# A linear attention product on two 64-row halves of the array, a value block in one piece, and one weight split on GpSimd

## What is computed

```python
# cross attention: the value and output weights are folded into one product
out = softmax(qp @ kp.T * scale) @ vp @ Wo.T
# linear attention, 16 heads of 32
q, k = relu(rmsnorm(q)), relu(rmsnorm(k))
kv = einsum('bhnd,bhne->bhde', k, v)
out = einsum('bhnd,bhde->bhne', q, kv)
out = out / (einsum('bhnd,bhd->bhn', q, k.sum(axis=2)) + eps)[..., None]
x = x + out @ W_out + b_out
# experts: 4 of 256 hidden columns
hid = silu(x @ Wg[e]) * (x @ Wu[e])
```

## Time and profile before

| | |
|---|---|
| median of 3 runs | 527.33 us (526.98 to 527.74) |
| the profiled execution | 527.25 us |
| its span | 525.1 us |
| TensorE busy | 520.9 us, 99% of the span |
| VectorE, ScalarE, GpSimd busy | 374.2, 243.3 and 245.3 us |

### The profile page before, as it was taken

One profiled execution on the slowest core, in us unless ns is written; L12 is line 12 of the kernel. 1 busy time (PEld: TensorE's weight loads), 2 busy tenths in 40 slices (PEclk: granted clock), 3 DMA queues, 4 the chain that ended last, 5 costly groups with the idle time before them and its releaser, 6 DMA issues.

```text
span 525.1 us, 6996 instructions
## 1 busy us (share of the span) xinstructions
PE 520.9 (99%) x2536; PEld 434.4 (83%) x2536; DVE 374.2 (71%) x615; ACT 243.3 (46%) x391; POOL 245.3 (47%) x159
## 2 busy tenths in 40 slices
PE   9999999999999999999999999999999999999997
PEld 8888888888888888888888888888888888988885
DVE  5673677876667766567878644999967477739996
ACT  4743434745535444453554534656645332562210
POOL 3735006331211322224244243338519948888993
PEclk9999999999999999999999999999999999999999
DMA  8721233232422223322232212242250312751102
GB/s 307 315 70 52 81 85 116 104 137 82 149 92 80 81 92 144 143 104 81 102 139 80 82 40 73 81 169 80 98 183 1 120 42 90 253 200 60 61 1 80
DMA packets 17607, 57.10 MB, mean 109 GB/s; under 512 B 2083, under 2 KB 2595, under 8 KB 16806
## 3 DMA queue, kind: packets, MB, share of 16 engines
q1 hardware_dynamic: 17286, 56.27, 30.5%
q10 hardware_dynamic: 288, 0.39, 0.2%
HBM read 54.55 MB, written 2.10 MB: 108 GB/s over the span
## 4 chain that ended last, share of the span: by engine, by line
PE 99%; DVE 0%; issue 0%; POOL 0%; POOLq 0%
PE bank L1463 28%; PE bank L1581 11%; PE bank L1592 11%; PE bank L1582 11%; PE bank L1594 11%; PE bank L1583 11%; PE bank L1593 11%; PE bank L1513 2%; PE bank L1453 1%; PE bank L1731 1%; PE bank L1474 1%; PE bank L1488 0%; PE bank L1720 0%; PE bank L1782 0%; DVE xs L1444 0%; PE bank L1749 0%
## 5 line engine op out<-in xcount | busy, mean ns | idle before, releaser
L575 POOL TENSOR_TENSOR cn_l<-raw_n,cn_h 128x1024 fp32r<-128x1024 f32 x32 | 77.7, 2428 | 185.5 <-ACT cn_h L757 185.5
L775 ACT COPY ring<-bank 128x512 f32<-128x512 f32 x64 | 37.7, 589 | 148.3 <-PE bank L1583 148.1
L1100 DVE TENSOR_TENSOR top<-top,bank 128x512 f32<-128x512 f32 x60 | 41.1, 685 | 86.4 <-ACT ring L775 86.3
L1581 PE MATMUL bank<-qk_h,ct_h 128*128 128x512 f32 x256 | 99.8, 390 | 0.0
L1583 PE MATMUL bank<-qk_h,ct_l 128*128 128x512 f32 x256 | 99.6, 389 | 0.0
L1582 PE MATMUL bank<-qk_l,ct_h 128*128 128x512 f32 x256 | 99.6, 389 | 0.0
L1592 PE MATMUL bank<-ph,cn_h 128*128 128x512 f32 x256 | 99.6, 389 | 0.0
L1593 PE MATMUL bank<-pl,cn_h 128*128 128x512 f32 x256 | 99.6, 389 | 0.0
L1594 PE MATMUL bank<-ph,cn_l 128*128 128x512 f32 x256 | 99.6, 389 | 0.0
L1581 PEld LDWEIGHTS bank<-qk_h,ct_h 128*128 128x128 f32 x256 | 48.0, 188 | 10.6 <-issue 0.8
L1583 PEld LDWEIGHTS bank<-qk_h,ct_l 128*128 128x128 f32 x256 | 48.1, 188 | 10.1
(11 more groups left out here) (248 smaller groups left out, 911.7 us busy)
## 6 DMA issues: line engine op xcount, KB each, us to landing
raw_t<-ctx_t SPq DMA_DIRECT2D x32, 512.0 KB, 4.2
raw_n<-ctx_n SPq DMA_DIRECT2D x32, 512.0 KB, 3.3
piece_raw<-pieces SPq DMA_DIRECT2D x12, 512.0 KB, 3.4
shifted<-xn_rows SPq DMA_DIRECT2D x12, 256.0 KB, 3.1
taps<-taps_in SPq DMA_DIRECT2D x1, 1280.0 KB, 7.5
xs<-x SPq DMA_DIRECT2D x4, 256.0 KB, 5.6
wq_raw<-wq_t SPq DMA_DIRECT2D x4, 256.0 KB, 6.3
wk_raw<-wk_in SPq DMA_DIRECT2D x1, 1024.0 KB, 7.9
```

What stands on the lines that cost most here:

```text
L575: pool.tensor_tensor(cn[p % CNB][1][:], raw_n[p % 2][:], cn[p % CNB][0][:].bitcast(F32), ALU.subtract).then_inc(cnl_ready, 1)
L1100: dve.tensor_tensor(top[:], top[:], bank[:, S_BANKS[i % 2], :], ALU.max).then_inc(max_done, 1)
L1581: pe.matmul(bank[:, dst, :], ct[i // 2 % 2][0][:, c, keys], qk[0][:, c, :], start=(c == 0), stop=False)
```

## The change

Three parts.

1. `low_wv(3)` leaves VectorE; the same subtraction stands on GpSimd behind `split_wo(3)` and ahead of the `wq` parts, with a semaphore of its own, `wv3_ready`, for which `fold_pass(3, 2)` waits.
2. The mask keeps two heads side by side instead of four: rows 0 to 63 of a chunk hold heads 0 and 1 in a block diagonal of 64 x 66, rows 64 to 127 heads 2 and 3. `linear` makes for each chunk two products of 64 rows and 66 columns, one in the upper and one in the lower half of the array's rows, into two different banks. The four mask multiplications become two. All of `linear` now stands ahead of the first transposition of `heads`. The output product of row block 0 gets an order of its own (`first_z`): the passes with the high part of the transposed rows first, the transposition of block 1 in their middle, the passes with the low part last. The output products get their own bank list, `Z_BANKS`.
3. In the experts, `values(1)` is made in one piece of 512 columns behind `gates(1, second)`; the second half of gate 0 has an order of its own (`second_gate`), high parts of the rows first; the last transposition of x2 stands behind three products of gate 1 instead of six.

```diff
@@ vector
-            low_wv(3)
@@ gpsimd, behind split_wo(3)
+            pool.wait_ge(wv_high, 3)
+            pool.tensor_tensor(wv[1][:, 3, :], wv_raw[:, 3, :], wv[0][:, 3, :].bitcast(F32),
+                               ALU.subtract).then_inc(wv3_ready, 1)
@@ gpsimd, the mask
-                pool.memset(kvmask[h * DH:(h + 1) * DH, h, :], 1.0).then_inc(masks_ready, 1)
+                pool.memset(kvmask[h * DH:(h + 1) * DH, h % 2, :], 1.0).then_inc(masks_ready, 1)
@@ banks
-        HEAD_BANKS = (2, 3, 0, 1)
+        HEAD_BANKS = (2, 1, 0, 1)
+        Z_BANKS = (3, 2, 0, 1)
@@ vector, the masks and heads
-            for c in range(C):
-                dve.wait_ge(kv_psum, c + 1)
-                dve.tensor_tensor(kv[:, c, :].rearrange("p (h w) -> p h w", h=HG),
-                                  bank[:, KV_BANKS[c], 0:HW].unsqueeze(1).to_broadcast([P, HG, HW]), kvmask[:],
-                                  ALU.mult).then_inc(kv_ready, 1)
+            for pair in range(2):
+                dve.wait_ge(kv_psum, 2 * pair + 2)
+                at_bank = KV_BANKS[2 * pair]
+                dve.tensor_tensor(kv[:, 2 * pair:2 * pair + 2, :].rearrange("p c (i w) -> p c i w", i=2),
+                                  bank[:, at_bank:at_bank + 2, 0:HW].unsqueeze(2).to_broadcast([P, 2, 2, HW]),
+                                  kvmask[:].unsqueeze(1).to_broadcast([P, 2, 2, HW]), ALU.mult).then_inc(kv_ready, 1)
...
-                for b in range(2):
-                    if t == 0 and b == 1:
-                        ins.then_inc(heads_ready, 1)
+                for r in range(2):
                     ins = dve.tensor_tensor(
-                        heads[:, t, b * 2 * P:(b + 1) * 2 * P].rearrange("p (g h e) -> p g h e", g=2, h=HG),
-                        la[:, b, :, :, 0:DH],
-                        rnorm[:, t, 2 * b:2 * b + 2, :].unsqueeze(3).to_broadcast([P, 2, HG, DH]), ALU.mult)
+                        heads[:, t, :].rearrange("p (c r i e) -> p r c i e", c=C, r=2, i=2)[:, r],
+                        la[:, r, :, :, 0:DH],
+                        rnorm[:, t, :, 2 * r:2 * r + 2].unsqueeze(3).to_broadcast([P, C, 2, DH]), ALU.mult)
@@ tensor, linear attention
-                for c in chunks:
-                    if t == 0:
-                        pe.wait_ge(kv_ready, c + 1)
-                    ins = pe.matmul(bank[:, LA_BANKS[t] + c // 2, c % 2 * VW:(c % 2 + 1) * VW],
-                                    qrT[:, c, t * P:(t + 1) * P], kv[:, c, :], start=True, stop=True)
+                for c in range(C):
+                    if t == 0 and c % 2 == 0:
+                        pe.wait_ge(kv_ready, c // 2 + 1)
+                    for r in range(2):
+                        two = slice(r * 2 * DH, (r + 1) * 2 * DH)
+                        ins = pe.matmul(bank[:, LA_BANKS[t] + r, c * 2 * HW:(c + 1) * 2 * HW],
+                                        qrT[two, c, t * P:(t + 1) * P], kv[two, c, :], start=True, stop=True,
+                                        tile_position=(r * 2 * DH, 0))
+                ins.then_inc(la_psum, 1)
...
+            def first_z(c, a, b):
+                return pe.matmul(bank[:, Z_BANKS[0], :], xT[a][:, c, 0:P], wout[b][:, c, :], start=(c == 0 and a == b),
+                                 stop=(c == C - 1 and a == 1))
+
+            pe.wait_ge(xh_ready, 3 * TT + 1)
+            for c in range(C):
+                if c == 2:
+                    transpose_heads(1)
+                first_z(c, 0, 0)
+                first_z(c, 0, 1)
+            pe.wait_ge(xl_ready, 3 * TT + 1)
+            for c in range(C):
+                ins = first_z(c, 1, 0)
+            ins.then_inc(z_psum, 1)
+            transpose_heads(2)
@@ tensor, experts
-            for half in ((0, 1), (2, 3)):
-                if half[0] > 0:
+            for some in ((0,), (1, 2, 3)):
+                if some[0] > 0:
                     transpose_x2(3)
...
-            values(1, first)
-            for m in range(2):
-                gates(m, second)
-                values(m, second)
...
+            pe.wait_ge(xh_ready, 5 * TT)
+            for c in range(C):
+                second_gate(c, 0, 0)
+                second_gate(c, 1, 0)
+            pe.wait_ge(xl_ready, 5 * TT)
+            for c in range(C):
+                ins = second_gate(c, 0, 1)
+            ins.then_inc(g_psum, 1)
+            values(0, second)
+            gates(1, second)
+            values(1)
```

More of the change, by code:

```diff
@@ L166, in perceiver_block @@
         key_bias, biased_max = (at(173.8125 + n / 16, f"by_32_{n}", [QB, TB]) for n in range(2))
-        kvmask = at(172.5, "kvmask", [P, HG, HW])
+        kvmask = at(172.5, "kvmask", [P, 2, HW])
         lower = at(173.25, "lower", [P, E, E])
@@ L183, in perceiver_block @@
         qrT = at(160, "qrT", [P, C, T])
-        kv = at(168.25, "kv", [P, C, VW])
+        kv = at(168.25, "kv", [P, C, 2 * HW])
         late = at(62, "late", [P, 512])
@@ L250, in perceiver_block @@
         wv_ready = sem("wv_ready")
+        wv3_ready = sem("wv3_ready")
         wv0_loaded = [sem(f"wv0_loaded{h}") for h in range(2)]
@@ L522, in _ @@
             pool.tensor_copy(wr[:, :, 0:E], wr_raw).then_inc(wr_ready, 1)
-            pool.wait_ge(wv_ready, C - 1)
+            pool.wait_ge(wv_ready, C - 2)
+            pool.wait_ge(wv3_ready, 1)
             pool.wait_ge(ctl_ready, 2)
@@ L1536, in _ @@
                     transpose_x(transposed_at[e, 1])
-                pe.wait_ge(wv_ready, e)
+                if e < C - 1:
+                    pe.wait_ge(wv_ready, e)
+                else:
+                    pe.wait_ge(wv3_ready, 1)
                 fold_pass(e, 2)
@@ L1724, in _, with linear @@
                             ins.then_inc(kv_psum, 1)
-            def linear(t, chunks=range(C)):
-                pe.wait_ge(qrT_ready, C)
-                for c in chunks:
-                    if t == 0:
-                        pe.wait_ge(kv_ready, c + 1)
-                    ins = pe.matmul(bank[:, LA_BANKS[t] + c // 2, c % 2 * VW:(c % 2 + 1) * VW],
-                                    qrT[:, c, t * P:(t + 1) * P], kv[:, c, :], start=True, stop=True)
[L1733 to L1738, removed]
-            def transpose_heads(t):
[L1742 to L1750, removed]
+            def linear(t):
+                for c in range(C):
[7 more added lines that the diff above has]
+                ins.then_inc(la_psum, 1)
+            pe.wait_ge(qrT_ready, C)
+            for t in range(TT):
+                linear(t)
+            def transpose_heads(t):
+                pe.wait_ge(heads_ready, t + 1)
+                transpose_tile(heads, t, HEAD_BANKS[t]).then_inc(xnT_psum, 1)
             def transpose_x2(t):
@@ L1756, in _ @@
             transpose_heads(0)
-            linear(2, (2, 3))
-            linear(TT - 1)
-            transpose_heads(1)
             pe.wait_ge(w2_ready, 2 * len(W2_ORDER))
-            for t in range(TT):
+            def first_z(c, a, b):
[12 more added lines that the diff above has]
+            transpose_heads(2)
+            for t in range(1, TT):
                 pe.wait_ge(xl_ready, 3 * TT + t + 1)
@@ L1768, in _ @@
                         transpose_x2(1)
-                    ins = project(HEAD_BANKS[t], [cut(xT, c, t * P, (t + 1) * P) for c in some],
+                    ins = project(Z_BANKS[t], [cut(xT, c, t * P, (t + 1) * P) for c in some],
                                   [cut(wout, c, 0, D) for c in some], starts=(some[0] == 0), stops=(some[0] > 0))
@@ L1834, in _, with second_gate @@
             pe.wait_ge(x2_ready, TT)
-            for half in ((0, 1), (2, 3)):
-                if half[0] > 0:
+            for some in ((0,), (1, 2, 3)):
+                if some[0] > 0:
                     transpose_x2(3)
-                project(1, [cut(expert("g", 0, C), c, P, 2 * P) for c in half],
-                        [cut(xT, c, 0, HALF) for c in half], cols=first, starts=(half[0] == 0), stops=(half[0] > 0))
-            values(1, first)
-            for m in range(2):
-                gates(m, second)
-                values(m, second)
+                project(1, [cut(expert("g", 0, C), c, P, 2 * P) for c in some],
+                        [cut(xT, c, 0, HALF) for c in some], cols=first, starts=(some[0] == 0), stops=(some[0] > 0))
+            def second_gate(c, a, b):
+                return pe.matmul(bank[:, 0, second], expert("g", 0, C)[a][:, c, 0:P], xT[b][:, c, second],
+                                 start=(c == 0 and a == b), stop=(c == C - 1 and b == 1))
+            pe.wait_ge(xh_ready, 5 * TT)
[9 more added lines that the diff above has]
+            values(1)
             route()
```

6 lines of the change are left out of this document (3 added, 3 removed).

## The result

The changed kernel takes 528.20 us (median; 527.54 to 528.78 over 22 runs), the kernel before 527.22 in the same runs. The ratio is 1.0019, with an interval of 1.0014 to 1.0025: 0.98 us slower, which is clear of no change and just under the 0.2% (1.05 us) that the forecast took as its line for "same". One execution of the kernel before took 1068.97 us, and the ratio leaves it out. The profiled execution took 528.13 us with a span of 525.9.

What follows compares the result with a forecast made beforehand. TensorE, busy 520.9 of 525.1 us, bounds the kernel. Start -0.15 and value block bring the sum to -0.31; linear attention adds 1.0, giving +0.7: 528.0 us against the median, range 526.3 to 530.0.

Steps and rivals of the forecast that it cites:

- the hole: Before the first output product, TensorE stands still about 0.8 us until ScalarE's copy of the transposed heads 0 ends.
- the moved transposition: Transposition of heads 1, formerly done before the first output product, now comes behind its start: 0.44 us lost.
- value block: Experts' second value block: 12 products of 512 columns replace twice 12 of 256, winning 0.16 us; last x2 transposition stays hidden.
- A round of two halves lasts as long as a load of 128 columns: Linear product: halves overlap, each hiding a load only up to its length; 32 rounds at about 0.11 us, 3.52 us; chance 0.50.
- the masks: In block 0 of the linear product, TensorE waits some 0.05 us for the second kv mask operation.
- short loads: Rival, linear product: loads in the halves are short or fully hidden, rounds of 0.059 us; 526.5 us in all; chance 0.18.
- loads in turn: Rival, linear product: the halves' 64 loads follow each other, 6.9 us; 531.3 us in all; chance 0.14.
- unhidden loads: Rival, linear product: a load isn't hidden behind its own half's product, 5.34 us; 529.8 us in all; chance 0.09.
- lower bound of 0.059 us a round: Linear product: a round takes only the shortened 66-column product's time, 1.89 us for all rounds.
- The first output product has to wait for ScalarE's copy: Output product of row block 0 starts 0.58 us later, waiting for ScalarE's copy of transposed heads 0.
- Leaving the halves: Return from half-array form before the heads transposition: about 0.12 us plus an uncovered load of 58 ns, 0.17 together.
- The start: Fourth row block: with the subtraction off VectorE, scaled rows come at about 16.4 and TensorE's 0.15 us wait is won.

Runs made afterwards that it cites:

- narrow halves: Changed kernel with linear products moving 33 columns instead of 66, heads 1 and 3 of each chunk left out; one run, 530.39 us.
- quarters: Changed kernel with each 64-row linear product cut into two of 64 stationary columns, four 64 x 64 tiles: 528.29 us; with heads 1 transposed first, 527.77.
- mixture: Changed kernel with linear row blocks 0 and 1 on 64 x 64 tiles, 2 and 3 on halves, heads 1 transposed first: 527.15 us, ratio 1.0003.
- the order on the whole array: Changed kernel with the linear product again on 128 rows, 132 columns and four masks, the changed order kept: 528.21 us, ratio 1.0019.

## Why the prediction was right

**The forecast** of 528.0 us held, and by the mechanism that it named: +0.98 us measured for the +0.7 foreseen, the hole and the moved transposition. Of the 0.28 us between the two, the profiles name 0.24: 0.09 in the stage, 0.06 in the value block, 0.09 in the long middle, which the change doesn't touch. That it came out as "same" is partly luck: 0.98 us lies just under the line of 1.05, and the interval reaches 1.0025. Point by point:

*A round of two halves lasts as long as a load of 128 columns.* Foreseen 3.72 us from the start to the last record, with 0.05 for the masks 3.77; it came to 3.78. The narrow halves show that it is not the columns moved that bound it, and the quarters that it is the columns of the load. The rivals with short loads (it would have been 2.2 us), with loads in turn (7.1) and with unhidden loads (5.5) are out. The price of 0.81 ns for each column moved, from which the forecast had its lower bound of 0.059 us a round, did not come back in the halves: with 33 columns a record there is no shorter than with 66, and no run shows a round that the columns moved would bound.

The Trainium skill ("TensorE: Matmul & The Clock Gate", section "LDWEIGHTS (loading the stationary operand)") says that the row count doesn't matter to a load. The trace agrees: 188 ns for 64 rows, 190 for 128. The Trainium skill's "TensorEngine Tiling (Array Packing)", section "Theoretical Speedup", gives up to twice the speed at 64 rows or fewer. The trace shows none of it here, 3.78 us for 3.80, under a load of 128 columns. The same page of the Trainium skill says, under "Key Properties", that changing the tiling mode drains the engine. The trace shows a price at the place, 0.15 us at each return to the whole array, and not what it is made of.

*The first output product has to wait for ScalarE's copy, and the transposition of heads 1 moves onto the path.* +0.58 and +0.44 foreseen, +1.11 measured, and by the starts in the timeline it is +0.65 and +0.46. The first output product started 5.13 us behind the linear one, where it had started at 440.25, 4.48 us behind it, before; from there to the first product of row block 1 it took 3.64 us where 3.18 were before. The forecast put the start of that product at 5.31 us, of which 0.16 is its allowance for the lag between a record's columns and its end. Without that it is 5.15, so every other term on this path was right together. The lag is the term that was too small: the overlap that the hole took away is 0.24 us.

*The hole:* foreseen "about 0.8 us, ended by ScalarE's copy", and it is 0.75 on the chain. *Leaving the halves:* foreseen 0.17, measured 0.60 - 0.44 = 0.16. *The masks:* foreseen 0.05; VectorE's second one ended at 435.95, and the ninth and the eleventh record of the product start 0.06 us later, together, than the pace of the rest gives.

*The start:* -0.15 foreseen and seen; the scaled rows came at 16.02, earlier than the 16.4 foreseen, and TensorE no longer waits for them. *The value block:* -0.16 foreseen, -0.10 seen; the 36 products behind `second_gate` took 5.63 us for 24 x 0.120 + 12 x 0.227 = 5.60. The last transposition of x2, asked for three products earlier, took 0.44 us as always: hidden, as was said.

**What I got wrong came in the experiments.** For the quarters I expected the rounds' gain in the time and got a pause of 1.1 to 1.3 us in its place; for the mixture 3.0 us and got 3.30. And I thought that the order on the whole array would come out a little under the changed kernel; it came out level (528.21 and 528.20), which the stage (8.91 and 9.02) puts at 0.1, too little to be measured.

**Open:** whether what TensorE waited for in the quarters were instructions, as the packet's times suggest, and what lets the clock fall in one execution and not in another.

## What to carry to other kernels

Before an array is cut into row halves, set the load of the weights beside the product that covers it: in these runs fewer rows did not shorten a load (188 ns for 190) and fewer columns did (133), and a product shortened below its load won nothing. What a rewrite of such a stage costs lies less in the array than in the order: a transposition, copied by another engine and then multiplied, needs as much unrelated TensorE work behind it as the copy takes (here a hole of 0.75 us in the chain), and a rewrite that moves this work away pays for it. The chain makes such a hole look cheaper than it is, by the overlap of two neighbours that it ends (here 0.24 us); compare starts. And before a profile is read, set its execution beside the others of the kernel: the one of the quarters was 1.3 us over the median. Two parts that win 0.25 us and one that loses 1.1 look like one change of +1; take the stage apart by one number from the chain, then keep the parts that win.

## What the runs showed that I had not expected

Products of 64 x 64 tiles, 66 columns wide, came at 58 ns for four tiles, eight instructions, and behind 116 of 128 product records TensorE stood still for 1.08 and 1.32 us in two kernels at the same place, until 1.51 us behind the end of an instruction packet both times. The kernels with 64 such records and then halves, and the changed kernel, are this many records (232, loads counted) into the stage only behind 441 us, long after their packets, which ended at 437.1 to 437.4; they have no pause. Small tiles thus had a second limit behind the load; that it is the supply of instructions fits all of this and is not shown.

The granted clock fell to 0.50 in two profiled executions whose TensorE never stood still in this part for more than 1.1 us. In the quarters it fell at 440.81, behind a pause and a hole; in the narrow halves at 438.71, ahead of the hole, with TensorE at work all the time before. The shape of the products alone does not explain it. The kernel before has none of these shapes, and two of its 81 executions beside the experiments (529.98 and 530.01) have a mean granted clock of 0.997 and 0.996; none of the 22 of the changed kernel went under 0.999. The quarters had it in 4 of 22 executions over two kernels. That thin or small products make the fall more likely may be; the narrow halves ran once, and the runs don't show it. At 0.50 four output products took 1.85 to 2.05 us for 1.16 and a transposition 0.85 for 0.44; the narrow halves lost 2.7 us of the stage to it that way (11.73 for 9.02).
